# First attention of a four-layer kernel: value step in column halves, and the split of the shifts on GpSimd

## The reference, cut to what matters

```python
q = (xn @ wq).reshape(bs, sl, h, hd).transpose(0, 2, 1, 3)
k = (xn @ wk).reshape(bs, sl, h, hd).transpose(0, 2, 1, 3)
v = (xn @ wv).reshape(bs, sl, h, hd).transpose(0, 2, 1, 3)
scores = jnp.einsum('bhid,bhjd->bhij', q, k)
probs = jax.nn.softmax(scores / jnp.sqrt(jnp.float32(HIDDEN_DIM)), axis=-1)
out = jnp.einsum('bhij,bhjd->bhid', probs, v)
out = out.transpose(0, 2, 1, 3).reshape(bs, sl, -1) + xn
```

## Time and profile before

| what | us |
|---|---|
| median of 3 runs | 1122.49 |
| lowest, highest run | 1117.06, 1125.56 |
| the profiled execution | 1121.55 |
| its span, first to last instruction | 1119.7 |
| first score of the first attention | 51.57 |
| last instruction of the first attention ends | 435.61 |

### The profile page before, as it was taken

One profiled execution on the slowest core, in us unless ns is written; L12 is line 12 of the kernel. 1 busy time (PEld: TensorE's weight loads), 2 busy tenths in 40 slices (PEclk: granted clock), 3 DMA queues, 4 the chain that ended last, 5 costly groups with the idle time before them and its releaser, 6 DMA issues. The chain is left out here.

```text
span 1119.7 us, 16494 instructions
## 1 busy us (share of the span) xinstructions
PE 969.5 (87%) x5528; PEld 526.3 (47%) x5528; DVE 754.5 (67%) x1302; ACT 663.3 (59%) x1437; POOL 384.6 (34%) x348
## 2 busy tenths in 40 slices
PE   4589889889889885896599999999999999579997
PEld 2222222222222222333467676776767676456665
DVE  6888888888888884325445454545455454768997
ACT  3377777777777775322355555555555543357887
POOL 4600000000000000000764938576584920336665
PEclk8699999999999998898799999999999999799999
DMA  3320000000000001000000000000000000000001
GB/s 66 141 90 17 21 15 18 20 15 19 19 15 19 18 1 27 1 0 15 0 1 10 1 5 11 1 1 6 10 1 6 1 1 1 14 8 17 15 18 45
DMA packets 23121, 19.92 MB, mean 18 GB/s; under 512 B 5448, under 2 KB 17712, under 8 KB 23048
## 3 DMA queue, kind: packets, MB, share of 16 engines
q1 hardware_dynamic: 23048, 18.99, 5.7%
HBM read 14.26 MB, written 4.59 MB: 17 GB/s over the span
## 5 line engine op out<-in xcount | busy, mean ns | idle before, releaser
L399 DVE TENSOR_REDUCE halves<-max_bank 128x2 f32<-128x1024 f32 x256 | 309.9, 1225 | 39.9 <-PE max_bank L541 32.0
L508 ACT ACTIVATE probs<-score_bank 128x512 f32<-128x512 f32 x512 | 267.5, 602 | 107.8 <-PE score_bank L579 107.7
L1144 ACT ACTIVATE a_probs<-a_scores,a_lowest 128x896 f32<-128x896 f32 (+7 forms) x128 | 94.9, 742 | 113.1 <-DVE a_lowest L1139 112.5
L1389 PE MATMUL a_sum<-a_turned,a_v 128*128 128x512 f32 (+3 forms) x384 | 158.5, 500 | 0.8 <-ACT a_headsT L1318 0.6
L579 PE MATMUL score_bank<-q_stack,k_stack 50*128 50x512 bf16 x512 | 133.2, 390 | 28.4 <-ACT probs L508 25.0
L592 PE MATMUL summed<-probs,v_tile 128*32 128x512 f32 x1024 | 137.2, 608 | 0.2 <-ACT probs L508 0.2
L541 PE MATMUL max_bank<-k_stack,q_stack 48*128 48x512 bf16 x512 | 114.8, 392 | 19.2 <-DVE halves L399 19.0
L1139 DVE TENSOR_REDUCE a_lowest<-a_scores 128x1 f32<-128x896 f32 (+7 forms) x128 | 96.2, 756 | 41.5 <-PE a_scores L1133 41.0
L579 PEld LDWEIGHTS score_bank<-q_stack,k_stack 50*128 50x128 bf16 x512 | 33.6, 93 | 186.7 <-ACT probs L508 141.9
L337 POOL COPY v_tile<-values 128x128 f32<-128x128 f32 x16 | 4.7, 296 | 337.8 <-PE summed L592 337.3
L1521 POOL TENSOR_TENSOR m_gated<-m_linear,m_sigm 128x512 f32<-128x512 f32 x64 | 87.6, 1370 | 49.5 <-ACT m_sigm L1616 49.5
(11 more groups left out here) (237 smaller groups left out, 1606.1 us busy)
## 6 DMA issues: line engine op xcount, KB each, us to landing
rope<-in_rope SPq DMA_DIRECT2D x1, 2048.0 KB, 9.4
m_w<-in_L_ffn_mlp_w SPq DMA_DIRECT2D x32, 64.0 KB, 1.8
q_parts<-l_q_parts SPq DMA_DIRECT2D x2, 768.0 KB, 4.9
k_parts<-l_k_parts SPq DMA_DIRECT2D x2, 768.0 KB, 6.3
q_stack<-q_parts SPq DMA_DIRECT2D x30, 48.0 KB
k_stack<-k_parts SPq DMA_DIRECT2D x30, 48.0 KB
x<-in_L_attn_x SPq DMA_DIRECT2D x2, 512.0 KB, 4.2
q_stack<-shift SPq DMA_DIRECT2D x64, 2.0 KB
```

What stands on the lines that cost most here:

```text
L399: dve.reduce_max(halves[:, u % 2, half, :].rearrange("p (x t) -> p x t", x=2)[:, :, qt], max_bank[place % RING][:, :, :], AX_X).then_inc(f ...
L508: act.activation(probs[:, k % PROBS, x, :], score_bank[e % SCORES][:, :], ACT.Exp, scale=SCALE0).then_inc(prob_ready, 1)
L1144: act.activation(probs[:, k % 2, c, 0:row_width(n)], scores[n % 2][:, 0:row_width(n)], ACT.Exp, bias=lowest[:, n % 8:n % 8 + 1], accum_out ...
L1389: pe.matmul(sum_bank[:, skipped(k, j):CH], v[:, BLOCKS[k][0], j, :], turned[:, m % SLOTS, skipped(k, j):CH], start=(j == 0), stop=(TURNED_ ...
```

## The change

The value step is cut into two halves of 256 queries each (`use(n)`), and one half is issued in every step, three steps (LAG) behind the scores. `probs` is six steps deep. The searches run 14 steps ahead (LEAD = TILES + 6). The turn follows the search of step 3; the fold goes ahead of the search of step 7. The last half block of a unit is issued in step 2 of the next one, while the take stays behind the exponentials of step 1 in ScalarE's queue. The split into high and low part moves ahead of the transpose and to GpSimd: three operations on 128x8 numbers (`split_maxima`); TensorE then transposes both parts at once (16 columns), and VectorE copies them out with one instruction. The sign moves to the rows of ones in the keys, which are now -1.

```diff
-LEAD = TILES + 4
-FOLD_AT = 6
+LEAD = TILES + 6
+TURN_AT = 3
+FOLD_AT = 7
...
-PROBS = 4
+PROBS = 6
+LAG = 3
...
+    if k == FOLD_AT and u >= 1:
+        yield "fold", u - 1
     if m < TILES * UNITS0:
         yield "search", m
-    if k == LEAD - TILES and u + 1 < UNITS0:
+    if k == TURN_AT and u + 1 < UNITS0:
         yield "turn", u + 1
-    if k == FOLD_AT and u >= 1:
-        yield "fold", u - 1
...
-                        pool.memset(stack[x * ROW + ROW // 2:(x + 1) * ROW, :], 1.0).then_inc(ones_set, 1)
+                        pool.memset(stack[x * ROW + ROW // 2:(x + 1) * ROW, :], -1.0).then_inc(ones_set, 1)
...
+                def split_maxima(u):
+                    pool.wait_ge(joined, u + 1)
+                    if u >= 1:
+                        pool.wait_ge(split, 3 * u)
+                    pool.tensor_copy(high16[:, u % 2, :], maxima[:, u % 2, :]).then_inc(split, 1)
+                    if u >= 2:
+                        pool.wait_ge(filled, PLACE["turn", u - 2] + 1)
+                    pool.wait_ge(split, 3 * u + 1)
+                    pool.tensor_copy(shift_parts[:, u % 2, 0, :], high16[:, u % 2, :]).then_inc(split, 1)
+                    pool.wait_ge(split, 3 * u + 2)
+                    pool.tensor_tensor(shift_parts[:, u % 2, 1, :], maxima[:, u % 2, :], high16[:, u % 2, :], ALU.subtract).then_inc(split, 1)
...
-                for pair in range(2, NPAIR):
-                    stage(pair)
+                for u in range(UNITS0):
+                    split_maxima(u)
+                    if u % 2 == 1 and u // 2 + 1 in range(2, NPAIR):
+                        stage(u // 2 + 1)
...
-                    mT = max_bank[place % RING][0:TILES, 0, 0:P]
-                    dve.tensor_scalar(shift[:, u % 2, 0, :], mT, -1.0, None, ALU.mult).then_inc(high_ready, 1)
-                    dve.wait_ge(high_ready, u + 1)
-                    dve.scalar_tensor_tensor(out=shift[:, u % 2, 1, :], in0=mT, scalar=-1.0, in1=shift[:, u % 2, 0, :],
-                                             op0=ALU.mult, op1=ALU.subtract).then_inc(freed, 1)
+                    dve.tensor_copy(shift[:, u % 2, :], max_bank[place % RING][0:2 * TILES, 0, 0:P]).then_inc(freed, 1)
...
-                    pe.wait_ge(joined, u + 1)
-                    pe.transpose(max_bank[place % RING][0:TILES, 0, 0:P], maxima[:, u % 2, :], t.identity[:, :]).then_inc(filled, 1)
+                    pe.wait_ge(split, 3 * u + 3)
+                    pe.transpose(max_bank[place % RING][0:2 * TILES, 0, 0:P], shift_parts[:, u % 2, :, :].rearrange("p a n -> p (a n)"), t.identity[:, :]).then_inc(filled, 1)
...
-                        last = pe.matmul(summed[VW * slot:VW * (slot + 1), :], v_tile[pair % 2][:, x, k, :], probs[:, k % PROBS, x, :],
-                                         start=(g == 0), stop=(g == GROUPS - 1), tile_position=(0, VW * slot))
-                    last.then_inc(used, 1)
+                        last = pe.matmul(summed[VW * slot:VW * (slot + 1), cols], v_tile[pair % 2][:, x, k, :], probs[:, (u * TB + k) % PROBS, x, cols],
+                                         start=(g == 0 and side == 0), stop=(g == GROUPS - 1 and side == 1), tile_position=(0, VW * slot))
+                    if side == 1:
+                        last.then_inc(used, 1)
...
-                        if k == 1 and u >= 1:
-                            use(u - 1, GROUPS - 1)
-                        if k % 2 == 1 and k >= 3:
-                            use(u, (k - 3) // 2)
...
+                    if step >= LAG:
+                        use(step - LAG)
+                for n in range(UNITS0 * TB - LAG, UNITS0 * TB):
+                    use(n)
```

More of the change, by code:

```diff
@@ L186, in layer0 @@
         maxima = sb("maxima", [P, 2, TILES])
-        shift = sb("shift", [TILES, 2, 2, P], BF16)
+        shift_parts = sb("shift_parts", [P, 2, 2, TILES])
+        shift = sb("shift", [2 * TILES, 2, P], BF16)
+        high16 = sb("high16", [P, 2, TILES], BF16)
         max_bank = [ps(f"max_bank{i}", [P, 2, CH]) for i in range(RING)]
@@ L207, in layer0 @@
         staged, padded_set, fold_set = sem("staged"), sem("padded_set"), sem("fold_set")
-        filled, freed, joined, high_ready = sem("filled"), sem("freed"), sem("joined"), sem("high_ready")
+        filled, freed, joined, split = sem("filled"), sem("freed"), sem("joined"), sem("split")
         score_ready, prob_ready, used = sem("score_ready"), sem("prob_ready"), sem("used")
@@ L274, in subtract @@
                         sp.dma_start(q_stack[pair % STACKS][row:row + ROW + 1:ROW, half * CH:(half + 1) * CH],
-                                     shift[:, u % 2, part, :]).then_inc(shift_in[u % 2], 16)
+                                     shift[part * TILES:(part + 1) * TILES, u % 2, :]).then_inc(shift_in[u % 2], 16)
                 load_x(0)
@@ L403, in search, with take_shift @@
                         if u >= 2:
-                            dve.wait_ge(filled, PLACE["turn", u - 2] + 1)
+                            dve.wait_ge(split, 3 * (u - 1))
                         dve.tensor_tensor(maxima[:, u % 2, :], halves[:, u % 2, 0, :], halves[:, u % 2, 1, :], ALU.max).then_inc(joined, 1)
-                def split(u, place):
+                def take_shift(u, place):
                     dve.wait_ge(filled, place + 1)
@@ L431, in take_ring @@
                     if what == "turn":
-                        split(n, PLACE[use])
+                        take_shift(n, PLACE[use])
                     if what == "fold":
@@ L498, in _ @@
                 mid(7)
-                for u in range(UNITS0):
-                    for k in range(TB):
-                        if u * TB + k >= PROBS and k % 2 == 0:
-                            done = (u * TB + k - PROBS) // 2 + 1
-                            act.wait_ge(used, done)
-                        for x in range(2):
-                            e = 2 * (u * TB + k) + x
-                            act.wait_ge(score_ready, e + 1)
-                            act.activation(probs[:, k % PROBS, x, :], score_bank[e % SCORES][:, :], ACT.Exp, scale=SCALE0).then_inc(prob_ready, 1)
-                        if k == 1 and u >= 1:
-                            take(u - 1)
+                for step in range(UNITS0 * TB):
+                    u, k = divmod(step, TB)
+                    if step >= PROBS and step % 2 == 0:
+                        done = (step - PROBS) // 2 + 1
+                        act.wait_ge(used, done)
+                    for x in range(2):
+                        e = 2 * step + x
+                        act.wait_ge(score_ready, e + 1)
+                        act.activation(probs[:, step % PROBS, x, :], score_bank[e % SCORES][:, :], ACT.Exp, scale=SCALE0).then_inc(prob_ready, 1)
+                    if k == 1 and u >= 1:
+                        take(u - 1)
                 take(UNITS0 - 1)
@@ L581, in score, with use @@
                               tile_position=(x * ROW, 0)).then_inc(score_ready, 1)
-                def use(u, g):
-                    pair = u // 2
-                    if g == 0:
+                def use(n):
+                    group, side = divmod(n, 2)
+                    u, g = divmod(group, GROUPS)
+                    pair, cols = u // 2, slice(side * CH // 2, (side + 1) * CH // 2)
+                    if g == 0 and side == 0:
                         pe.wait_ge(staged, pair + 1)
@@ L609, in _ @@
                     give_ring(event)
-                for u in range(UNITS0):
-                    for k in range(TB):
-                        for x in range(2):
-                            score(u, k, x)
-                        for event in ring_of_step(u, k):
-                            give_ring(event)
-                        if k == 1 and u >= 1:
-                            use(u - 1, GROUPS - 1)
-                        if k % 2 == 1 and k >= 3:
-                            use(u, (k - 3) // 2)
-                use(UNITS0 - 1, GROUPS - 1)
+                for step in range(UNITS0 * TB):
+                    u, k = divmod(step, TB)
+                    for x in range(2):
+                        score(u, k, x)
+                    for event in ring_of_step(u, k):
+                        give_ring(event)
+                    if step >= LAG:
+                        use(step - LAG)
+                for n in range(UNITS0 * TB - LAG, UNITS0 * TB):
+                    use(n)
                 give_ring(("fold", UNITS0 - 1))
```

3 lines of the change are left out of this document (2 added, 1 removed).

## The result

| | before | changed |
|---|---|---|
| median | 1120.95 us (20 runs) | 1127.11 us (20 runs) |
| ratio changed to before | | 1.0063, 95% interval 1.0045 to 1.0080 |
| profiled execution | 1121.55, span 1119.7 | 1123.33, span 1121.5 |
| first turn | 44.56 | 49.57 |
| first score | 51.57 | 54.46 |

The changed kernel is 0.63% slower, 6 to 7 us. The forecast was no change that a measurement tells, 1121; it lies inside 1%, but with an interval wholly on the slow side. The "take of unit 28" is the 29th of 32, and an "undisturbed unit" is one without a fall of the clock or a late transfer. The table is read from row to row: the difference grows from 2.9 us at the first score to 4.4 at the first take and 5.7 at the 29th, and shrinks to 5.1 at the end of the stage.

The account below looks back on a forecast made before the run. The prediction took engines waiting on each other in turn, none full, as the bound. It summed +2.2 (start) - 29 x 0.06 (units) - 1.7 (end) = -1.2 us, giving a forecast of 1121 us, range 1102 to 1136.

Parts of the forecast that it names:

- The unit: One period of the engines' loop in the first attention: forecast 11.92 us, against 11.98 before.
- Half block 0.57: TensorE's value step on 256 queries: 0.43 us streaming plus 0.14 fixed, against 1.00 for a full block.
- wait at step 3: TensorE's score of step 3, second head, waits 1.28 us for an exponential queued behind the take on ScalarE.
- a hidden fixed part (0.50): Rival: a half block takes 0.50 us, saving 0.5 us a unit, 14 us in all, about 1106; chance 0.20.
- VectorE's 10.7: Rival: the unit reaches VectorE's own 10.7 us, 38 us less in all, about 1083; chance 0.08.
- the uncovered weights (0.68): Rival: each half block's second pass waits for weights, 0.68 us; +22 us in all, about 1142; chance 0.15.
- The removed instruction: VectorE's second split instruction, 0.28 us: removal worth nothing, since the bank's refill keeps that stretch at 0.49.
- GpSimd's operations in the unit: Three small split operations: 1.0 us, at most 2.2, against 1.77 us of cover; add nothing to the sum.
- The start: First split waits behind GpSimd's residual operation; first score at 54.7 instead of 51.57, 3.1 us late.
- Balance +2.2: Net cost at the start in us: first score 3.1 late, less 0.9 won back by unit 0 at 11.5.
- The end: From unit 30's first score to the last divide: 22.6 us instead of 24.3, ScalarE setting the pace; gain 1.7.
- The chance of 0.60: Chance given to a time within about 1% of before; faster had 0.26 and slower 0.14.

Follow-up runs that it names:

- the take experiment: Changed kernel with ScalarE's take of the previous unit behind the exponentials of step 2 instead of step 1: 1094.65 us, ratio to before 0.9778.
- Moving the split alone: Changed kernel with GpSimd's split of unit 0 ahead of the third residual operation, not behind it: 1121.7 us, ratio to before 1.0018.
- the early split: Changed kernel with unit 0's split ahead of the third residual operation, and the take behind step 2's exponentials: 1089.93 us, ratio to before 0.9739.
- search first: Changed kernel with TensorE issuing the search ahead of the two scores in step 3: 1108.8 us, ratio to before 0.9880.
- whole blocks: Changed kernel with whole value blocks of 512 columns, issued in steps 1, 3, 5 and 7: 1134.98 us, ratio to before 1.0134.
- split on VectorE, later take: Changed kernel with the split as two VectorE instructions again and the take behind step 2's exponentials: 1091.81 us, ratio to before 0.9745.
- split on VectorE, take as changed: Changed kernel with the split as two VectorE instructions again, order, halves and buffers as changed: 1130.87 us, ratio to before 1.0082.

## Why the prediction was right and wrong

*The unit.* Forecast 11.92 against 11.98, measured 11.89. Half block 0.57, as forecast; wait at step 3 of 1.3, measured 1.28; ScalarE idle 0.9 ahead of the take, measured 0.87. The rivals of a hidden fixed part (0.50), of VectorE's 10.7 and of the uncovered weights (0.68) all fall. That TensorE's new work and the take's wait eat what VectorE wins was right, and the take experiment shows it from the other side: with the wait gone the changed order takes 10.94, 1.0 us a unit less than before.

*The removed instruction.* Forecast worth nothing behind the ring's refill: right, shown in both orders (11.89 and 10.94 with either). What the forecast did not look at is the queue of transfers behind it: with two instructions the loads of a pair come 0.3 us later, and the profile has 2.3 us of longer units.

*GpSimd's operations in the unit.* Forecast 1.0 us and covered; measured 0.79 from first start to last end, and the turn follows 1.0 later.

*The start.* This term was mis-sized. "The first score at 54.7" was right (54.46), but "It wins back 0.9. Balance +2.2" was not. Unit 0, from its first score to that of unit 1, takes 13.22 (54.46 to 67.68), where 11.5 was forecast and the kernel before has 12.42 (51.57 to 63.99): it loses 0.8 more, and the balance is +3.7. The forecast had two steps with a half block at TensorE's lower clock; there are three, and the first of them, with the turn in it, takes 3.4 us (scores at 57.86, 61.25, 63.23, 65.21). The clock came back at 65.8 in this execution, against 59.3 before, 11.3 us behind the first score and not 7.8. Moving the split alone is worth 4 to 5 us.

*The end.* "Gain 1.7" did not come: from unit 30's first score to the last divide are 24.46 us (416.23 to 440.69), against 24.34 before, so +0.1. The step took ScalarE as running without a gap. But the fold, a full 1.00 of TensorE, leaves it idle 0.96 in unit 30, the take's wait stands in unit 31 too (0.59 of ScalarE), and behind the last exponential come 4.2 us, not 3.6.

*The step that is missing.* The sum had no term for the clock, since the earlier trace rows showed 1.00; it took the level of before for a property of the stage. The changed order puts TensorE to rest for 0.9 us in one stretch, and then the clock falls now and then, 1.5 us a time. In the profiled execution that is 3.0 us, and filling the wait gives 3 to 5 back. A sum of the profiled execution by the forecast's own marks closes: up to unit 1's first score +3.7; 29 units at -0.08, -2.4; two falls +3.0; two smaller irregular units (12.20, the first, which every profile of this loop has 0.3 or more long, and 12.23) +0.65; end +0.1: 5.1, measured 5.1. The forecast of -1.2 differs by 1.5 at the start, 3.0 for the falls and 1.8 at the end; in the units between, the 0.02 that a unit is shorter than forecast and the two irregular ones cancel.

The range, 1102 to 1136, holds the time, since it was wide for the half block's cost, which was right; it was not made for the clock. A small gain was forecast and a loss clear of noise came. The chance of 0.60 on a change below 1% came out, with a true loss inside it.

## What to carry to other kernels

Where two engines feed each other, follow one period of the loop from row to row; here that gave the unit to 0.03 us, while busy shares said nothing. When a piece of work is cut and moved later, look for what drains it in another engine's queue and move that along: one line (take behind step 2) turned a loss of 0.6% into a gain of 2.2%, and with the early split 2.6%. When helper work moves to another engine, look at what that engine has queued at the start of the stage, not only in its steady part. And look at what stands behind a result in the queue of transfers: a removed instruction that wins nothing where it stood can still send later loads earlier.

## What the runs showed that I had not expected

- A pause of 0.89 us of TensorE in every unit of 11.89 us came with falls of the granted clock to 0.50, of about 3.4 us each, in all four profiles that had it; with three redundant matmuls of 0.22 us in the pause there was none, and the kernel was 3 to 5 us faster though it did more work. A pause of 0.67 (search first) and waits of 0.31 to 0.45 (before, whole blocks) came with none. Why one unit of many is hit stays open.
- The clock's return after the start differs by 6 us between two kernels whose first scores are within 0.2 us: 60.8 (split on VectorE, later take) and 66.5 (split on VectorE, take as changed); and by 10 between two with the first score near 54.4: 65.8 (changed) and 75.9 (whole blocks). What decides it stays open.
- The small GpSimd operations on 128x8 take 0.19 to 0.20 us each, and their starts are 0.32 and 0.27 apart, waits included.
